# Gated attention and a three-layer sign network: layer three as seven products of half blocks, three of its weight sums on GpSimd

## The chip, the cores and the metric

The kernel runs on one core of one Trainium2 chip. The metric is device time in microseconds for the whole program, the median of several executions. Beside them one execution was profiled; every row below is from that one. The engines are TensorE (PE, its weight loads PEld), VectorE (DVE), ScalarE (ACT), GpSimd (POOL) and SyncE (SP), which issues nearly all DMAs here. Each takes its own instructions strictly in order and is tied to the others by semaphores.

## The reference

The input x is 4096 tokens of 512 features (2 x 2048), the context 256 keys (2 x 128). In short:

```python
x = x + tanh(g_xattn) * attention(layernorm(x), ctx, ctx)      # 16 heads of 32, 128 keys
h = concatenate([y, -y])                                       # y = layernorm(x)
h = 2 * relu(s0 * h @ sign(k0))                                # 1024 -> 2048
h = 2 * relu(s1 * h @ sign(k1))                                # 2048 -> 2048
out = x + tanh(g_ffn) * s2 * h @ sign(k2)                      # 2048 -> 512
```

The three weight matrices hold only +1 and -1 (from booleans), so they and small sums of them are exact in fp8. Activations are split into two fp16 parts, high and low, and each product is two matmuls into the same bank.

## The kernel before

Tokens go in 16 chunks of 256 (`CHUNKS`), of two tiles of 128 (`TT`). For a chunk f, layer one (L0) makes 2048 rows of H in 8 pairs (`PAIRS`), layer two ("L1", 2048 x 2048, weights W1) works in 4 groups (`GROUPS`) of 512 outputs, and layer three ("L2", 2048 x 512, weights W2) adds each group's share into two output banks. While chunk f goes through the network, the attention of chunk f+1 is woven in: `SLOTS` lists the steps of a chunk in order, and `WEAVE` and `QUERIES` say after which slot an attention item comes. Every engine walks through the same list and does its own part of each slot, first the slot's (`feed`), then the woven items (`attend`). So the list is the order of the work on all engines, written by hand.

From chunk 1 on, layer two is computed by a seven-product scheme (Strassen's, in Winograd's form): a group of 512 outputs times 256 tokens is split in 2 x 2 blocks; seven products P1, P2, P6, P5, P7, P4, P3 of half blocks (32 matmuls of 128 columns each, L1255 and L1256) replace eight. Its sums of weights (S1 to S4) are made once on VectorE in `weight_step` (L983 to L997); its sums of activations are made for each pair in layer one (L870 to L875, after which ScalarE makes the high part, `pair_hi`, L618, and VectorE the low one, `pair_lo`, L839). Its results are gathered in C11, C12 and C22: ScalarE copies a running bank (`take`, L622), VectorE adds another bank (`add`, L844), ScalarE rectifies into the high part of h1 (L667, L677, L680, L685) and VectorE makes the low part (`h1_rest`, L852). TensorE may only add on to a bank when the copy of it is done (`l1_copy`).

Layer three is plain before: for each group and half of the group's tiles (`second_feed`, L1272 and L1273), 8 matmuls of 512 columns, 64 a chunk; two banks (3 and 4) hold the output of the two token tiles over the whole chunk, and `finish` (L907) adds them to the kept x once a chunk. The share of the last group falls into the next chunk's slots (L2P).

An attention item S is the scores of 4 heads (L1167): VectorE takes the maximum (L804), ScalarE the exponents (4 instructions, L529), and in item PS its high part (L607), VectorE the low part (L808), SyncE sends both through a DMA transpose. PV is the product with the values (L1132, L1133), VectorE scales it (L815, L817) and GpSimd adds its two halves (L476). CT, WO, N2, T2 are the output projection and the second layernorm, LN, N1, T1 the first layernorm of the chunk after next, Q and QS the queries. Items use banks 5 to 7 in turn.

The order that ties an item to its neighbours on an engine:

```python
for f in range(CHUNKS):
    for s, slot in enumerate(SLOTS):
        feed(slot, f)
        ...
        if f < CHUNKS - 1:
            for ahead, item in woven(s, f):
                attend(item, f + ahead)
```

## Time and profile before

| | us |
|---|---|
| median of 3 runs | 1567.62 (1564.46 to 1568.11) |
| the profiled execution | 1564.91 |
| its span, first to last instruction | 1563.1 |
| TensorE busy | 1518.9 (97%), 19872 matmuls, granted clock 1.00 |
| VectorE busy | 940.2 (60%) |
| ScalarE busy | 673.7 (43%) |
| GpSimd busy | 168.7 (11%) |
| chunk 7, first layer-one matmul to that of chunk 8 | 92.66 |

A row such as `L839 DVE TENSOR_TENSOR H<-Fp,H 128x896 f16<-128x896 f32 x120 | 130.1, 1084 | 0.0` is a group of instructions: line, engine, operation, what it writes and reads, shapes, count, then busy us and mean ns of one, then the idle time before them and who ended it. In a timeline the first number is the start in us, the second the duration. Instructions of one engine overlap in their fill and drain, so the distance from start to start is shorter than the duration: for throughput one reads the starts. A matmul's duration is modelled and far longer than its distance to the next.

### The profile page before, as it was taken

How to read it: one execution, taken by the hardware profiler on the slowest of the kernel's cores; microseconds unless marked ns; L12 is line 12 of the kernel's file. 1: busy time of each engine (PE TensorE's matmuls, PEld its weight loads, DVE VectorE, ACT ScalarE, POOL GpSimd, SP SyncE). 2: the span in 40 equal slices, each digit the busy share in tenths (PEclk: the TensorE clock that was granted, in tenths of full speed). 3: DMA queues.
4: the chain of work that ended last, by engine and by line, in shares of the span. 5: the costliest groups of instructions: out<-in, count | busy, mean ns of one | idle time of the engine just before them, and what ended most of it. 6: DMA issues, size and time to landing. Idle time of an engine off the chain costs nothing.

```text
span 1563.1 us, 46137 instructions
## 1 busy us (share of the span) xinstructions
PE 1518.9 (97%) x19872; PEld 1297.3 (83%) x19872; DVE 940.2 (60%) x1938; ACT 673.7 (43%) x1568; POOL 168.7 (11%) x273
## 2 busy tenths in 40 slices
PE   6798999999999999999999999999999999999999
PEld 4586888888888888898988888888898888889887
DVE  5877766756556565655656566465655656565442
ACT  3452452635435253452535445263553525345231
POOL 2202001010100102011020200101010010201000
PEclk9999999999999999999999999999999999999999
DMA  9443232342424333252443524333242443424100
GB/s 256 127 104 58 46 95 62 89 70 62 90 52 101 65 85 78 50 100 55 96 69 71 93 44 103 62 89 69 62 90 52 101 67 83 78 50 100 29 29 15
DMA packets 278227, 120.96 MB, mean 77 GB/s; under 512 B 243464, under 2 KB 259848, under 8 KB 277896
## 3 DMA queue, kind: packets, MB, share of 16 engines
q1 hardware_dynamic: 275960, 117.48, 34.6%
q8 instruction: 157, 2.57, 0.7%
q10 hardware_dynamic: 2064, 0.53, 0.1%
q14 instruction: 46, 0.38, 0.1%
HBM read 37.76 MB, written 16.78 MB: 35 GB/s over the span
## 4 chain that ended last, share of the span: by engine, by line
PE 80%; DVE 8%; ACT 6%; issue 3%; DMA 2%; POOL 0%; SPq 0%; ACTq 0%; DVEq 0%; POOLq 0%
PE bank L1255 19%; PE bank L1256 19%; PE bank L1222 7%; PE bank L1223 7%; PE bank L1272 6%; PE bank L1273 6%; ACT Pf L529 3%; DVE nmax L804 2%; PE bank L1139 2%; PE bank L1141 2%; PE bank L1140 2%; PE bank L1123 2%; PE bank L1124 2%; PE bank L1125 2%; DMA PT<-Phl 1%
## 5 line engine op out<-in xcount | busy, mean ns | idle before, releaser
L1255 PE MATMUL bank<-H,W 128*128 128x128 f16 x6720 | 778.3, 219 | 5.7 <-ACT C L622 4.4
L1256 PE MATMUL bank<-H,W 128*128 128x128 f16 x6720 | 778.0, 219 | 0.0
L1255 PEld LDWEIGHTS bank<-H,W 128*128 128x128 fp8e5 x6720 | 655.3, 98 | 18.1 <-ACT C L622 10.2
L1256 PEld LDWEIGHTS bank<-H,W 128*128 128x128 fp8e5 x6720 | 657.4, 98 | 7.1
L1222 PE MATMUL bank<-hT,W 128*128 128x256 f16 x1024 | 226.8, 273 | 3.5 <-DVE hT L745 1.9
L1223 PE MATMUL bank<-hT,W 128*128 128x256 f16 x1024 | 226.8, 273 | 0.0
L529 ACT ACTIVATE Pf<-bank,nmax 128x128 f32<-128x128 f32 x512 | 146.4, 368 | 137.1 <-DVE nmax L804 135.4
L1273 PE MATMUL bank<-W,h 128*128 128x512 fp8e5 x504 | 191.0, 379 | 0.0
L1272 PE MATMUL bank<-W,h 128*128 128x512 fp8e5 x504 | 191.0, 379 | 0.0
L476 POOL TENSOR_TENSOR attn<-pvs 128x128 f32<-128x128 f32 x120 | 75.0, 625 | 1002.9 <-DVE pvs L817 1002.9
L844 DVE TENSOR_TENSOR C<-bank,C 128x256 f32<-128x256 f32 x180 | 76.3, 424 | 159.4 <-ACT C L622 87.8
L622 ACT ACTIVATE C<-bank 128x256 f32<-128x256 f32 x180 | 69.9, 388 | 211.3 <-PE bank L1256 211.3
L808 DVE SCALAR_TENSOR_TENSOR Phl<-Pf,Phl 128x512 f16<-128x512 f32 x120 | 82.6, 688 | 93.5 <-ACT Phl L607 93.5
L839 DVE TENSOR_TENSOR H<-Fp,H 128x896 f16<-128x896 f32 (+1 forms) x128 | 135.3, 1059 | 0.8 <-ACT H L613 0.8
L647 ACT ACTIVATE Fp<-bank 128x512 f32<-128x512 f32 x128 | 76.5, 597 | 90.0 <-PE bank L1223 88.7
L618 ACT ACTIVATE H<-Fp 128x896 f16<-128x896 f32 x120 | 113.4, 945 | 1.8 <-DVE Fp L875 1.7
L852 DVE SCALAR_TENSOR_TENSOR h<-C,h 128x256 f16<-128x256 f32 x180 | 77.3, 430 | 60.7 <-ACT h L685 29.0
L1222 PEld LDWEIGHTS bank<-hT,W 128*128 128x128 fp8e5 x1024 | 100.2, 98 | 15.4 <-issue 4.0
L1223 PEld LDWEIGHTS bank<-hT,W 128*128 128x128 fp8e5 x1024 | 100.2, 98 | 11.4
L804 DVE TENSOR_REDUCE nmax<-bank 128x4 f32<-128x512 f32 x128 | 87.6, 684 | 17.3 <-PE bank L1167 16.3
L1273 PEld LDWEIGHTS bank<-W,h 128*128 128x128 f16 x504 | 49.3, 98 | 50.4
L1272 PEld LDWEIGHTS bank<-W,h 128*128 128x128 f16 x504 | 49.3, 98 | 50.5
(133 smaller groups left out, 1910.3 us busy)
## 6 DMA issues: line engine op xcount, KB each, us to landing
Qst<-q_bounce SPq DMA_DIRECT2D x120, 128.0 KB, 2.8
Y<-in_x_dram SPq DMA_DIRECT2D x16, 512.0 KB, 3.9
R<-X SPq DMA_DIRECT2D x16, 512.0 KB, 3.5
q_bounce<-Qhl SPq DMA_DIRECT2D x120, 64.0 KB
out_dram<-R SPq DMA_DIRECT2D x15, 512.0 KB, 2.6
W<-in_L_ffn_k_dram SPq DMA_DIRECT2D x8, 512.0 KB, 8.1
W<-in_L_ffn_k_dram SPq DMA_DIRECT2D x2, 1024.0 KB, 19.3
PT<-Phl SPq DMA_TRANSPOSE x120, 3.1
```

What stands on the lines that cost most here:

```text
L529: last = nc.scalar.activation(Pf[:, n % 2, j * P:(j + 1) * P], bank[:, j * P:(j + 1) * P], ACT.Exp, bias=nmax[:, n % 2, j:j + 1], scale=1.0)
L618: nc.scalar.activation(H0[:, 0, i], Fp[:, i % 3, 1:8, :], ACT.Copy).then_inc(l0_hi, 1)
L804: V_.tensor_reduce(nmax[:, n % 2, :], bank[:, :].rearrange("p (j k) -> p j k", j=4), AX.X, ALU.max, negate=True).then_inc(s_max, 1)
L808: V_.scalar_tensor_tensor(out=Phl[:, n % 2, 1, :], in0=Pf[:, n % 2, :], scalar=PS, in1=Phl[:, n % 2, 0, :], op0=ALU.mult, op1=ALU.subtract)\
L839: V_.tensor_tensor(H0[:, 1, i, rows, :], Fp[:, i % 3, of, :], H0[:, 0, i, rows, :], ALU.subtract)\
L852: V_.scalar_tensor_tensor(out=h1_part(q, half, late, 1), in0=source, scalar=0.0, in1=h1_part(q, half, late, 0), op0=ALU.max, op1=ALU.subtr ...
L1222: mm(o, w, hT[:, k, :], start=k == 0, stop=False)
L1223: last = mm(o, w, hT[:, KT + k, :], start=False, stop=k == KT - 1)
L1255: mm(o, w, H0[:, 0, i, b_of, :], start=first, stop=False, skip_group_check=True)
L1256: last = mm(o, w, H0[:, 1, i, b_of, :], start=False, stop=i == PAIRS - 1, skip_group_check=True)
L1272: mm(banks[3 + t][:, :], hi, w2, start=q == 0 and h == 0 and jj == 0, stop=False)
L1273: last = mm(banks[3 + t][:, :], lo, w2, start=False, stop=q == GROUPS - 1 and h == 1 and jj == 1)
```

## The change

Layer three takes the seven-product form too. From chunk 1 on, the outputs of layer two are kept as seven blocks of sums (h1 becomes `[P, 2, 2, 2, 7, HALF]`), and a pass over two groups is seven steps (`PASS`) of 8 matmuls of 256 columns (`third_step`). Passes stand in the new list of slots: pass 1 of a chunk (groups 2 and 3) among the next chunk's layer-one slots 4 to 15, pass 0 (groups 0 and 1) in slots 31 to 42 between layer-two steps. After a step VectorE adds one or two halves of the bank to the kept x (`add_up`, 8 reads a pass), in place of `finish`. For each group VectorE makes three sums (`group_sums`) at the end of the group, ScalarE the high parts (`group_hi`, 1280 and 512 elements) and VectorE the low parts (`group_lo`) at the start of the next group, all in two of the three Fp buffers that layer one uses. Within a group the last two products change places (P3, P4), C12 gets a second add, and the three banks rotate from group to group (`ROLES`). W2 gets 7 blocks; of its four sums three are made by GpSimd (`third_sum`: S3, S2, S4, each 2048 elements a partition) at slots 12 to 14 of chunk 1 in GpSimd's own order, and S1 by VectorE at slot 17 (`third_first`). In chunk 0 layer three stays plain, and in the last chunk for its last two groups.

To make room, Kst holds the keys of one batch at a time (restacked at the start of chunk 7), Pf has one buffer instead of two, attn shares xn, Qf shares pvs, and ident shares C11. The woven items move to new slots.

```diff
     STEPS = [(A_L11, B_R11, A, True), (A_L12, B_R21, B, True), (A_S2, B_T2, A, False),
-             (A_S1, B_T1, C, True), (A_S3, B_T3, A, False), (A_L22, B_T4, A, False),
-             (A_S4, B_R22, C, False)]
-    P1, P2, P6, P5, P7, P4, P3 = range(7)
+             (A_S1, B_T1, C, True), (A_S3, B_T3, A, False), (A_S4, B_R22, B, True),
+             (A_L22, B_T4, A, False)]
+    P1, P2, P6, P5, P7, P3, P4 = range(7)
+    ROLES = [[(q + role) % 3 for role in range(3)] for q in range(GROUPS)]
+    H_R11, H_R22, H_T1, H_T3, H_T2, H_R21, H_T4 = range(7)
+    EARLY_ROWS, LATE_ROWS = slice(0, 5), slice(5, 7)
+    PASS = [(A_L11, H_R11), (A_L12, H_R21), (A_S2, H_T2), (A_S1, H_T1), (A_S3, H_T3), (A_S4, H_R22), (A_L22, H_T4)]
+    PASS_BANK = [3, 4, 3, 4, 3, 4, 3]
+    READS = [(P1, 0, 1), (P2, 0, 1), (P6, 0, 0), (P5, 1, 0), (P5, 0, 0), (P7, 1, 0), (P3, 0, 0), (P4, 1, 1)]
+    PASS_NEEDS = [0, 0, 1, 2, 3, 5, 6]
+    READ_NEEDS = [0, 1, 0, 0, 3, 4, 5, 0]
+    PLAIN_FEED = {0: {0: (0, 0), 1: (0, 1), 3: (1, 0), 4: (1, 1)}, 1: {0: (2, 0), 1: (2, 1), 2: (3, 0), 3: (3, 1)}}
...
+    LAST_FEED = [(0, 1, 0), (1, 0, 1), (0, 0, 2), (1, 1, 3)]
+    SLOTS = [("L0", i, 0) for i in range(4)]
+    for n in range(4):
+        SLOTS += [("L2", 1, n), ("L0", 4 + n, 0)]
+    SLOTS += [("L2", 1, P7), ("L2", 1, P3), ("L1", 0, P1), ("L2", 1, P4)] + [("L1", 0, s) for s in range(P2, 7)]
+    SLOTS += [("L1", 1, s) for s in range(7)] + [("L1", 2, P1), ("L1", 2, P2)]
+    for n, s in enumerate((P6, P5, P7, P3)):
+        SLOTS += [("L2", 0, n), ("L1", 2, s)]
+    SLOTS += [("L2", 0, P7), ("L2", 0, P3), ("L1", 2, P4), ("L2", 0, P4)] + [("L1", 3, s) for s in range(7)]
...
+    for u, (scores, values) in enumerate(((14, 20), (17, 22), (19, 24), (21, 26), (23, 28), (25, 31), (27, 33),
+                                          (29, 36))):
+        weave(scores, "S", u)
+        weave(scores + 1, "PS", u)
+        weave(values, "PV", u)
     for t in range(TT):
-        weave(28 + 2 * t, "CT", t)
-        weave(31 + 2 * t, "WO", t)
-        weave(32 + 2 * t, "N2", t)
-        weave(33 + 2 * t, "T2", t)
-    weave(31, "LOAD", 0)
+        weave(34 + 3 * t, "CT", t)
+        weave(40 + 2 * t, "WO", t)
+        weave(41 + 2 * t, "N2", t)
+        weave(42 + 2 * t, "T2", t)
...
+    THIRD_SUMS = {12: 1, 13: 2, 14: 3}
...
-        W2 = sb("W2", [P, FT, D], f8)
+        W2 = sb("W2", [P, 7, PAIRS, D // 2], f8)
...
+            def third_sum(step):
+                L11, L12, L21, L22 = (W2[:, b] for b in range(4))
+                if step == 1:
+                    pool.wait_ge(w2_made, 1)
+                    pool.tensor_tensor(W2[:, A_S3], L11, L21, ALU.subtract, saturate=False).then_inc(w2_sums, 1)
+                if step == 2:
+                    pool.wait_ge(w2_sums, 1)
+                    pool.tensor_tensor(W2[:, A_S2], L22, W2[:, A_S3], ALU.subtract, saturate=False)\
+                        .then_inc(w2_sums, 1)
+                if step == 3:
+                    pool.wait_ge(w2_sums, 2)
+                    pool.wait_ge(l2_done, 2 * GROUPS)
+                    pool.wait_ge(w2_first, 1)
+                    pool.tensor_tensor(W2[:, A_S4], L12, W2[:, A_S2], ALU.subtract, saturate=False)\
+                        .then_inc(w2_sums, 1)
...
+            def group_hi(q, f):
+                for n, rows in enumerate((EARLY_ROWS, LATE_ROWS)):
+                    act.wait_ge(h2_step, 3 * group(f, q) + 2 + n)
+                    if n == 0:
+                        act.wait_ge(*pass_free(f, q))
+                    nc.scalar.activation(h1[:, q % 2, 0, :, rows, :], Fp[:, 1:3, rows.start + 1:rows.stop + 1, :],
+                                         ACT.Copy).then_inc(h2_hi, 1)
...
-                        take(n, s, f, C11, A)
+                        if n > 0 and not late(f, n - 1):
+                            group_hi(n - 1, f)
+                        if late(f, n - 1):
+                            act.wait_ge(h1_lo, NH + 1)
+                        take(n, s, f, C11)
...
+            def group_sums(q, f):
+                done = 3 * group(f, q)
+                Fg = Fp[:, 1:3]
+                dve.wait_ge(h2_relu, 3 * group(f, q) + 3)
+                V_.tensor_tensor(Fg[:, :, 3:5, :], Fg[:, :, 1:3, :], Fg[:, :, 0:1, :].to_broadcast([P, 2, 2, HALF]),
+                                 ALU.subtract).then_inc(h2_step, 1)
+                dve.wait_ge(h2_step, done + 1)
+                V_.tensor_tensor(Fg[:, :, 5, :], Fg[:, :, 4, :], Fg[:, :, 1, :], ALU.add).then_inc(h2_step, 1)
+                dve.wait_ge(h2_step, done + 2)
+                dve.wait_ge(l1_copy, copied(f, q, 3))
+                V_.tensor_tensor(Fg[:, :, 7, :], Fg[:, :, 6, :], Fg[:, :, 5, :], ALU.subtract).then_inc(h2_step, 1)
+            def group_lo(q, f):
+                for n, rows in enumerate((EARLY_ROWS, LATE_ROWS)):
+                    dve.wait_ge(h2_hi, 2 * group(f, q) + n + 1)
+                    V_.tensor_tensor(h1[:, q % 2, 1, :, rows, :], Fp[:, 1:3, rows.start + 1:rows.stop + 1, :],
+                                     h1[:, q % 2, 0, :, rows, :], ALU.subtract).then_inc(h2_lo, 1)
+            def add_up(f, p, s):
+                base = NR * passes(f, p)
+                for n, (step, half, tile) in enumerate(READS):
+                    if step != s:
+                        continue
+                    if n == 0 and p == 0:
+                        dve.wait_ge(r_copied, nth(f, 16, 15))
+                    if READ_NEEDS[n]:
+                        dve.wait_ge(l2_sum, base + READ_NEEDS[n])
+                    dve.wait_ge(l2_step, 7 * passes(f, p) + s + 1)
+                    rest = R[:, tile, half * CHUNK:(half + 1) * CHUNK]
+                    V_.scalar_tensor_tensor(out=rest, in0=banks[PASS_BANK[s]][:, 0:CHUNK], scalar=fin, in1=rest,
+                                            op0=ALU.mult, op1=ALU.add).then_inc(l2_sum, 1)
...
+                    if s == P4 and not late(f, n):
+                        group_sums(n, f)
...
+            def third_first():
+                V_.scalar_tensor_tensor(out=W2[:, A_S1], in0=W2[:, 2], scalar=-1.0, in1=W2[:, 3], op0=ALU.mult,
+                                        op1=ALU.subtract, saturate=False).then_inc(w2_first, 1)
...
-                        pe.wait_ge(l1_sum, nth(f - 1, NC, 3 * (n - 1) + 2))
+                        pe.wait_ge(l1_copy, copied(f, n, 0))
...
                     if s == P7:
-                        pe.wait_ge(l1_copy, nth(f - 1, NC, 3 * n + 1))
+                        pe.wait_ge(l1_copy, copied(f, n, 1))
...
+            def third_step(f, p, s):
+                base = NR * passes(f, p)
+                block, row = PASS[s]
+                if s == P1 and base == 0:
+                    pe.wait_ge(out_ready, NT)
+                elif s == P1:
+                    pe.wait_ge(l2_sum, base)
+                if PASS_NEEDS[s]:
+                    pe.wait_ge(l2_sum, base + PASS_NEEDS[s])
+                if f == 1 and p == 0 and s == P6:
+                    pe.wait_ge(w2_sums, 2)
+                if f == 1 and p == 0 and s == P5:
+                    pe.wait_ge(w2_first, 1)
+                if f == 1 and p == 0 and s == P3:
+                    pe.wait_ge(w2_sums, 3)
+                if s in (P1, P2):
+                    pe.wait_ge(h2_lo, 2 * group(f, 2 * p + 1) + 1 + s)
+                for q in (2 * p, 2 * p + 1):
+                    for i in range(2):
+                        for hl in range(2):
+                            last = mm(banks[PASS_BANK[s]][:, 0:CHUNK], h1[:, q % 2, hl, i, row, :],
+                                      W2[:, block, 2 * q + i, :],
+                                      start=s in (P1, P2, P5, P3) and q == 2 * p and i == hl == 0,
+                                      stop=q == 2 * p + 1 and i == hl == 1, skip_group_check=True)
+                last.then_inc(l2_step, 1)
...
+                    if kind == "L2" and f - q >= 1:
+                        third_step(f - q, q, h)
+                    if kind == "L2" and f - q == 0 and h in PLAIN_FEED[q]:
+                        second_feed(*PLAIN_FEED[q][h], 0)
```

## Rows read from the trace of the kernel before

**Rows 1.** The page, busy time: us (share of the span) x instructions.

```profile
PE 1518.9 (97%) x19872; PEld 1297.3 (83%) x19872; DVE 940.2 (60%) x1938; ACT 673.7 (43%) x1568; POOL 168.7 (11%) x273
```

**Rows 2.** Busy time by stretch: us, then each engine; chunk 7 and chunk 1.

```profile
734.57:753.79 19.22, 19.22 (x180) 17.22 (x178) 14.91 (x33) 12.95 (x22) 0.00 (x0) 1.00 0.15 42
757.23:785.59 28.36, 28.05 (x469) 25.80 (x468) 15.73 (x34) 14.42 (x42) 2.57 (x4) 1.00 0.57 109
734.57:827.23 92.66, 92.35 (x1259) 79.62 (x1257) 55.37 (x118) 41.94 (x98) 9.79 (x16) 1.00 0.41 77
175.37:269.39 94.02, 92.67 (x1256) 79.65 (x1257) 63.61 (x120) 41.67 (x97) 9.81 (x16) 1.00 0.33 77
```

**Rows 3.** The waits of TensorE: waited for, us in total, times, longest.

```profile
PE bank L1255 <- ACT C L622: 4.4, 15, 0.6
```

**Rows 4.** Groups by line and form, whole run: busy, mean ns, idle before.

```profile
L1273 PE MATMUL bank<-W,h 128*128 128x512 fp8e5 x504 | 191.0, 379 | 0.0
...
L839 DVE TENSOR_TENSOR H<-Fp,H 128x896 f16<-128x896 f32 x120 | 130.1, 1084 | 0.0
...
L618 ACT ACTIVATE H<-Fp 128x896 f16<-128x896 f32 x120 | 113.4, 945 | 1.8 <-DVE Fp L875 1.7
...
L446 POOL TENSOR_TENSOR X<-Y,bo_b 128x512 f32<-128x512 f32 x32 | 40.5, 1267 | 0.4 <-DVE bo_b L950 0.4
...
L987 DVE TENSOR_TENSOR W<-W 128x2048 fp8e5<-128x2048 fp8e5 x4 | 9.1, 2284 | 0.0
```

**Rows 5.** Timeline of TensorE, four places: start us, us, instruction.

```profile
72.10 0.27 PE L1223 MATMUL bank<-hT,W 128*128 128x256 f16 x1
72.20 0.27 PE L1222 MATMUL bank<-hT,W 128*128 128x256 f16 x1
...
706.40 0.38 PE L1272 MATMUL bank<-W,h 128*128 128x512 fp8e5 x1
706.62 0.38 PE L1273 MATMUL bank<-W,h 128*128 128x512 fp8e5 x1
...
762.82 0.39 PE L1167 MATMUL bank<-Kst,Qst 128*128 128x128 f16 x4
763.04 0.22 PE L1255 MATMUL bank<-H,W 128*128 128x128 f16 x1
...
766.61 0.39 PE L1167 MATMUL bank<-Kst,Qst 128*128 128x128 f16 x4
```

**Rows 6.** Timeline with GpSimd; then line 792 by tile (ns min/median/max).

```profile
783.94 0.42 DVE L817 TENSOR_TENSOR pvs<-bank,rden 128x256 f32<-128x256 f32 x1
784.28 0.68 DVE L808 SCALAR_TENSOR_TENSOR Phl<-Pf,Phl 128x512 f16<-128x512 f32 x1
784.44 0.83 POOL L476 TENSOR_TENSOR attn<-pvs 128x128 f32<-128x128 f32 x1 [5.29 <-DVE pvs L817]
784.88 0.69 DVE L804 TENSOR_REDUCE nmax<-bank 128x4 f32<-128x512 f32 x1
...
L792 DVE TENSOR_TENSOR xs<-attn,xs x30: 679/693/1083, 140.4 to 1451.1; 128x512 f16<-128x512 f32 x30
```

**Rows 7.** Timeline of VectorE and ScalarE around two score blocks.

```profile
763.73 0.68 DVE L804 TENSOR_REDUCE nmax<-bank 128x4 f32<-128x512 f32 x1
764.45 1.14 ACT L529 ACTIVATE Pf<-bank,nmax 128x128 f32<-128x128 f32 x4 [0.99 <-DVE nmax L804]
765.63 0.63 ACT L607 ACTIVATE Phl<-Pf 128x512 f16<-128x512 f32 x1
766.29 0.69 DVE L808 SCALAR_TENSOR_TENSOR Phl<-Pf,Phl 128x512 f16<-128x512 f32 x1 [1.87 <-ACT Phl L607]
...
774.10 1.14 ACT L529 ACTIVATE Pf<-bank,nmax 128x128 f32<-128x128 f32 x4 [1.09 <-DVE nmax L804]
775.12 0.40 ACT L622 ACTIVATE C<-bank 128x256 f32<-128x256 f32 x1
775.38 0.66 ACT L607 ACTIVATE Phl<-Pf 128x512 f16<-128x512 f32 x1
```

374 lines of the change are left out of this document (219 added, 155 removed).

## Prediction

> **What bounds the kernel now.** I read the busy table first [rows 1], then busy time by stage [rows 2], then who made TensorE wait [rows 3]. One steady chunk (chunk 7) takes 92.66 us and TensorE is busy for 92.35 of them; the 13 chunks from 2 to 14 are alike. TensorE is the bound. In the whole run its waits on ScalarE for a layer-two copy come to 4.4 us; I count 0.25 a chunk. So every matmul column that goes is worth its time, as long as VectorE and ScalarE still keep up. They look idle over a chunk (55 and 42 us of 92.66), but the stages differ: in the layer-one stretch VectorE is busy 14.91 of 19.22 us, and in the stretch with the scores it and ScalarE do 15.73 and 14.42 of 28.36 us, largely one after the other [rows 2].
>
> **What the change removes from TensorE.** Layer three is 64 matmuls of 512 columns a chunk (1024 in all, half of them in the row of L1273 and the rest in its twin and the tail) [rows 4]. One follows the other after 0.22 us (0.2156 over a long stretch) [rows 5]. A seven-product pass over two groups is 7 steps of 8 matmuls of 256 columns; such matmuls follow each other after 0.11 us (0.1091) [rows 5]. That they move fp8 weights changes nothing that the 512-column rows show. So 64 x 0.2156 = 13.80 us becomes 112 x 0.1091 = 12.22: 1.58 us less in each of chunks 1 to 14, and half of that in chunk 15; chunk 0 stays plain. 14 x 1.58 + 0.8 = **22.9 us less**.
>
> **What it adds, and by what price.** Start to start, without a wait: VectorE 0.34 us for 256 elements and 0.60 for 512 [rows 6], for 896 it lasts 1.08 [rows 4], start to start some 0.08 less as in the others, 1.00; so I estimate 1.40 for 1280. ScalarE: 0.26 to 0.3 for 256 [rows 7], and from 0.94 us for 896 [rows 4] about 1.16 for 1280 and 0.53 for 512. For each group VectorE loses four rests of 0.34 and gains one add (0.34), three group sums (0.73, 0.46, 0.36 with their hand-overs: 1.55), group_lo (1.40 + 0.60 = 2.0) and four reads of a product out of PSUM (4 x 0.36); finish goes (1.2 a chunk). That is 14 us more per chunk: 55 becomes about 69 of 91, still under TensorE. ScalarE gains group_hi, 1.16 + 0.53 = 1.69 a group, 7 us a chunk. By totals alone both would hide. Where they stand in the order decides.
>
> **The layer-one stretch** (slots 0 to 13). TensorE now needs 8 x 16 matmuls (1.745 us each time) for layer one, 4 x 12 (1.31) for the queries and 7 x 8 (0.87) for layer three, all of 256 columns: 25.3 us up to the end of the third step there. VectorE needs group_lo 2.0, eight pairs at 2.0, four query rests at 0.36, seven reads at 0.36: 22 us, but starts only when ScalarE has done group_hi, about 2 us in. Followed in order, the last low half of H is there 0.15 us before TensorE asks for it. I put it at nothing, with up to 1 us a chunk as upper bound; nothing to be gained. The cover is gone in chunk 15, where the queries (5.2 us) aren't there: 1 us net.
>
> **The score stretch** (slots 14 to 31), the heart of the forecast. A score block is a chain over both engines, read in [rows 7]: maximum to exponents 0.72 (763.73 to 764.45), exponents to their copy 1.18, copy to the low half 0.66, and 0.60 for that [rows 6]. If other work of ScalarE stands behind the exponents, it starts 1.02 after them (774.10 to 775.12). A step of layer two is 1.785 us, a score 0.22 (762.82 to 763.04; 762.82 to 766.61 is one score and two steps) [rows 5], a value product about 0.25 (8 matmuls of 65 columns, 0.03 each by the same pace).
> First wait: after score 3 (slot 21) VectorE does the group sums (1.55), then the maximum (0.73), ScalarE the exponents (1.02), and only then, since group_hi stands ahead of the copy of C11 in slot 22, group_hi (1.69) and the copy with its signal (0.38): 5.4 us. The product P6 in slot 24 adds to the bank that is copied and waits for it. TensorE has 2 steps, a score and a value product until there, 4.04 us. **1.35 us of waiting.**
> Second: from the start of group_hi, its first half (1.3), group_lo (2.0), the value scaling (0.55), the low half of score 3 (0.60), the add of C11 (0.34), the maximum of score 4 (0.73), exponents (1.02) and the copy of C12 (0.4) are 6.95 us; TensorE is through P6 and P5 6.15 us after that same start. P7 waits **0.8 us**.
> Third: two more score blocks take 3.65 and 4.0 us, about TensorE's own pace (4.04 for two slots), so nothing is caught up. After score 6 come its exponents (1.75), the rectified copy (0.45), the group sums (1.55), a value scaling (0.55), the low half (0.60) and the first part of group_lo (1.5): 6.4 us. The first step of layer three for groups 0 and 1 (slot 31) reads that part. TensorE gets there first by **2.05 us**.
> After slot 31 the layer-three steps and the output projection stretch TensorE's side, and I find no further wait above 0.1 us. Sum: 4.2 us a chunk, against 0.25 before [rows 3]. Bounds: 2.5 if each new long operation is a fifth cheaper than I took it, 5.0 if dearer. 13 x (4.2 - 0.25) = **51.4 us more**. The new waits of TensorE hold back the whole queue behind them, scores included, and VectorE, which depends on that queue, gains nothing by them.
>
> **Chunk 1 and the weight sums.** It now takes 94.02 us, 1.6 of that waits [rows 2]. VectorE's own sum for layer three (slot 17) and the layer-two weight sums in slots 13 and 25 stand in the same chain, each 2.3 us by the 2048-element row [rows 4]; by the same walk some 5.5 us of them come out on top of 4.2. 9.7 - 1.65 = **8 us more**. The three sums on GpSimd: its 512-element sum takes 1.27 us [rows 4], so 2048 elements are at most 5.1 us, 15 us in all. Two can start in chunk 0, right behind the last layernorm (GpSimd waits for no slot); the third waits for slot 17 of chunk 1 and is wanted in slot 40, over 30 us later. TensorE never waits for them. What is queued behind the third is the first value sum, wanted by VectorE four slots on; covered. But the two engines stop each other: a GpSimd sum beside VectorE's low half took 0.83 us [rows 6] and ended 0.39 after that one had drained, and a VectorE subtraction that takes 0.69 took up to 1.08 [rows 6]. If every GpSimd sum held VectorE for its whole length it would be 15 us, if it waited for gaps 0; I take **2 us**, nearest to the 0.4 of these rows, a few times. The Trainium skill ("GPSIMD Engine Reference", section Specifications) says that GpSimd's SBUF interface is shared with VectorE and contended when VectorE has two SBUF inputs; the rows agree. Its section "Performance versus the Vector engine" gives 4.5 us for a two-input addition over 2048 elements, twice VectorE's time, and advises against moving such work there; by its figure the three would be 13.5 us of GpSimd, once, and the forecast would stay.
>
> The rest is at nothing: the keys stacked for one batch at a time (the second batch goes out at the start of chunk 7, 14 slots ahead of its first score), W2 in two loads of the size of the layer-two loads, the shared buffers (Pf alone, since the low half of one score precedes the next maximum on VectorE anyway). Chunk 0's order changes with stalls of about 8 us in it; 3 either way.
>
> **Sum.** The profiled execution is 1564.9 us with its span of 1563.1; the median of the runs is 2.7 above, 0.2%. 1564.9 - 22.9 + 51.4 + 8 + 2 + 1 = 1604.4; I say 1605.
>
> **Rivals.** (a) All is covered: the hand-overs are shorter than the chain I built from single rows, and TensorE goes through. 1564.9 - 22.9 = 1542, with a few us of chunk 1 about 1545. For it: both engines have over 20% of idle time, and in the kernel before the same chain leaves TensorE 0.25 us of waiting a chunk. Against it: it does so with no sums and no group_hi or group_lo between the scores. (b) Half of it: only about half of the 4.2 us is seen, the waits being one slack spent once: some 1573. The break-even is at 1.8 us of waiting a chunk, and below it the sign turns. (c) More: VectorE also binds in the layer-one stretch by 1 us a chunk, or GpSimd holds it: 1620 to 1635. (d) The columns don't come back (256-column steps with overhead of their own, each step closed by a signal): at most 0.05 us a step, 10 us; within (b) or (c).
>
> **Chances.** My case 0.60 (1590 to 1618), (a) 0.20, (b) 0.10, (c) 0.10. Below 1546 I leave about 0.1, above 1622 about 0.08. About 0.3% (5 us) is what a measurement of this kernel can tell from no change. Faster 0.20 is (a); same 0.05 and slower 0.05 share (b); with my case and (c), slower is 0.75.
>
> **What would show it.** In the profile after, TensorE's matmul count and busy time in a chunk fall by the layer-three share while its chunk is 94 to 96 us long; its waits name ScalarE's copy of C (before P6 and P7 of the second group) and VectorE's group_lo (before the first step of layer three), each once a chunk, of 1.3, 0.8 and 2 us. Wrong if the steady chunk is near 91 us, if those waits are absent, or if the longest wait names W2.

## The result and the profile after

The kernel after takes **1647.2 us** (median of 4 runs, 1646.8 to 1648.4), the kernel before beside it 1567.3 us. The ratio is **1.0514** (interval 1.0496 to 1.0533), 80 us more. The forecast was 1605. The profiled execution of after has a span of 1645.5 us, 82.4 more than that of before.

First the page's busy times, then groups of the view by line and form: those of the layer-three products, of the reads out of PSUM (L1004), of group_lo (L989) and of group_hi (L736).

```profile
PE 1518.5 (92%) x20568; PEld 1374.8 (84%) x20568; DVE 1162.9 (71%) x2262; ACT 762.9 (46%) x1684; POOL 201.7 (12%) x276
...
L1458 PE MATMUL bank<-W,h 128*128 128x256 fp8e5 x1624 | 207.5, 274 | 28.7 <-DVE h L989 28.2 <-DVE R L1004 0.5
L1004 DVE SCALAR_TENSOR_TENSOR R<-bank,c,R 128x256 f32<-128x256 f32 x232 | 107.0, 477 | 15.9 <-PE bank L1458 15.6
L989 DVE TENSOR_TENSOR h<-Fp,h 128x1280 f16<-128x1280 f32 x58 | 89.6, 1545 | 46.9 <-ACT h L736 46.9
L736 ACT ACTIVATE h<-Fp 128x1280 f16<-128x1280 f32 x58 | 73.7, 1270 | 18.3 <-DVE Fp L981 18.3
L989 DVE TENSOR_TENSOR h<-Fp,h 128x512 f16<-128x512 f32 x58 | 39.6, 682 | 0.0
L736 ACT ACTIVATE h<-Fp 128x512 f16<-128x512 f32 x58 | 36.0, 620 | 0.0
```

TensorE's share fell from 97% [rows 1] to 92%: it is no longer the bound throughout. VectorE has 223 us more. Next, busy time by stretch, cut where layer one of each chunk begins: of after the prologue, chunks 0, 1, 7, 8 and 15.

```profile
0.00:74.75 74.75, 49.45 (x329) 35.69 (x330) 48.60 (x114) 28.14 (x73) 18.21 (x35) 0.95 0.69 190
74.75:184.35 109.60, 91.92 (x841) 76.01 (x841) 86.98 (x113) 36.05 (x81) 17.85 (x18) 0.96 0.33 68
184.35:293.52 109.17, 95.56 (x1280) 82.99 (x1281) 76.72 (x134) 45.57 (x103) 15.45 (x17) 0.98 0.26 61
780.44:877.30 96.86, 91.68 (x1304) 84.28 (x1305) 69.89 (x140) 48.16 (x107) 11.61 (x16) 1.00 0.38 78
877.30:975.32 98.02, 92.98 (x1304) 85.93 (x1305) 69.80 (x140) 48.11 (x107) 11.64 (x16) 0.98 0.35 72
1556.99:1645.50 88.51, 84.16 (x1171) 76.30 (x1168) 45.12 (x90) 28.16 (x51) 0.00 (x0) 1.00 0.05 20
```

And of before the three of these stretches that [rows 2] doesn't have: prologue, chunk 0, chunk 15.

```profile
0.00:71.77 71.77, 46.54 (x328) 34.57 (x329) 48.47 (x114) 28.15 (x73) 18.25 (x35) 1.00 0.72 197
71.77:175.37 103.60, 95.72 (x856) 77.52 (x857) 80.62 (x113) 36.10 (x81) 14.13 (x16) 1.00 0.36 76
1477.23:1563.10 85.87, 81.78 (x1107) 70.30 (x1104) 31.22 (x66) 23.49 (x45) 0.00 (x0) 1.00 0.05 20
```

So the 82.4 us lie here: prologue +3.0, chunk 0 +6.0, chunk 1 +15.2, chunks 2 to 14 +55.6 (4.3 each), chunk 15 +2.6. The last number but two of a row is the granted clock. It was 1.00 in every stretch of the profiled execution of before (all but one of the other runs of before whose clock was noted have a mean of 0.996 to 0.998); in after it is 0.95 to 0.98 in the first three rows and in chunks 2, 4, 8, 10 and 12, which last 98.0 us (chunk 10 98.7). Below, an undisturbed chunk is one at clock 1.00 without the odd longer wait for a transfer; several of each kernel agree within 0.05 us, in after at 96.4.

TensorE's waits, in the columns of [rows 3]:

```profile
PE bank L1430 <- ACT C L719: 35.4, 44, 3.2
PE bank L1458 <- DVE h L989: 28.2, 14, 2.6
PE bank L1396 <- DVE h L1010: 13.0, 1, 13.0
PE bank L1396 <- DVE C L962: 9.9, 13, 0.8
```

The first two are the forecast ones: copies of C by ScalarE, and group_lo by VectorE before layer three. The third is a single wait, ahead of chunk 1. The fourth, of each chunk's first step on the last add of C, was not forecast. In the timeline of TensorE in chunk 7 a wait is seen so; the number in brackets is the idle time:

```profile
823.69 0.39 PE L1341 MATMUL bank<-Kst,Qst 128*128 128x128 f16 x4
825.27 0.23 PE L1430 MATMUL bank<-H,W 128*128 128x128 f16 x1 [1.20 <-ACT C L719]
...
842.33 0.38 PE L1458 MATMUL bank<-W,h 128*128 128x256 fp8e5 x2 [1.86 <-DVE h L989]
...
876.32 0.22 PE L1431 MATMUL bank<-H,W 128*128 128x128 f16 x1
877.30 0.27 PE L1396 MATMUL bank<-hT,W 128*128 128x256 f16 x1 [0.76 <-DVE C L962]
```

Without a wait the step after a score starts 0.22 us after it [rows 5]; here it is 1.58, so 1.36 us are lost and not the 1.20 in the brackets. The idle time is counted from the modelled end of the last matmul, so each wait costs some 0.16 us more than it (0.25 idle in before's chunk 7 is 0.42 start to start). Below, "lost" is start to start, less the usual distance.

### The profile page after: what moved, and what is told of

Its sections match the earlier page's. It is cut to its first block, busy times and chain, and to the rows that moved or that the text cites. A ratio compares the mean times of both kernels' runs of the same rounds, so it can differ in the third digit from the quotient of the medians.

```text
span 1645.5 us, 48159 instructions
## 1 busy us (share of the span) xinstructions
PE 1518.5 (92%) x20568; PEld 1374.8 (84%) x20568; DVE 1162.9 (71%) x2262; ACT 762.9 (46%) x1684; POOL 201.7 (12%) x276
## 3 DMA queue, kind: packets, MB, share of 16 engines
q8 instruction: 162, 2.65, 0.7%
## 4 chain that ended last, share of the span: by engine, by line
PE 55%; DVE 22%; ACT 10%; issue 7%; POOL 3%; DMA 2%; SPq 0%; DVEq 0%; ACTq 0%; POOLq 0%
PE bank L1458 10%; PE bank L1430 10%; PE bank L1431 10%; PE bank L1396 6%; PE bank L1397 6%; ACT Pf L623 4%; DVE nmax L922 3%; DVE h L989 3%; DVE Phl L926 2%; DVE C L962 2%; PE bank L1313 2%; PE bank L1315 2%; PE bank L1314 2%; PE bank L1297 2%; ACT xs L688 2%
## 5 line engine op out<-in xcount | busy, mean ns | idle before, releaser
L1430 PE MATMUL bank<-H,W 128*128 128x128 f16 x6720 | 790.9, 220 | 38.1 <-ACT C L719 35.4
L1431 PE MATMUL bank<-H,W 128*128 128x128 f16 x6720 | 790.2, 220 | 0.0
L1396 PE MATMUL bank<-hT,W 128*128 128x256 f16 x1024 | 230.5, 274 | 24.8 <-DVE h L1010 13.0
L1458 PE MATMUL bank<-W,h 128*128 128x256 fp8e5 x1624 | 207.5, 274 | 28.7 <-DVE h L989 28.2
L1397 PE MATMUL bank<-hT,W 128*128 128x256 f16 x1024 | 230.5, 274 | 0.0
L551 POOL TENSOR_TENSOR xn<-pvs 128x128 f32<-128x128 f32 x120 | 72.1, 601 | 1031.0 <-DVE pvs L935 1031.0
L1458 PEld LDWEIGHTS bank<-W,h 128*128 128x128 f16 x1624 | 154.0, 98 | 47.7 <-issue 30.2
L962 DVE TENSOR_TENSOR C<-bank,C 128x256 f32<-128x256 f32 x240 | 100.4, 418 | 106.2 <-ACT C L719 53.2
L989 DVE TENSOR_TENSOR h<-Fp,h 128x1280 f16<-128x1280 f32 x116 | 124.5, 1114 | 46.9 <-ACT h L736 46.9
L728 ACT ACTIVATE Fp<-C 128x256 f32<-128x256 f32 x174 | 72.8, 418 | 133.3 <-DVE C L962 133.3
L1004 DVE SCALAR_TENSOR_TENSOR R<-bank,c,R 128x256 f32<-128x256 f32 x232 | 107.0, 477 | 15.9 <-PE bank L1458 15.6
L736 ACT ACTIVATE h<-Fp 128x1280 f16<-128x1280 f32 x116 | 103.8, 945 | 18.3 <-DVE Fp L981 18.3
```

Source lines behind the costliest of these rows:

```text
L962: V_.tensor_tensor(to[:, :, :], banks[bank][:, 0:CHUNK].rearrange("p (j n) -> p j n", j=2), to[:, :, :], ALU.add).then_inc(l1_sum, 1)
L989: V_.tensor_tensor(h1[:, q % 2, 1, :, rows, :], Fp[:, 1:3, rows.start + 1:rows.stop + 1, :], h1[:, q % 2, 0, :, rows, :], ALU.subtract).th ...
L1004: V_.scalar_tensor_tensor(out=rest, in0=banks[PASS_BANK[s]][:, 0:CHUNK], scalar=fin, in1=rest, op0=ALU.mult, op1=ALU.add).then_inc(l2_sum, 1)
L1396: mm(o, w, hT[:, k, :], start=k == 0, stop=False)
L1397: last = mm(o, w, hT[:, KT + k, :], start=False, stop=k == KT - 1)
L1430: mm(o, w, H0[:, 0, i, b_of, :], start=first, stop=False, skip_group_check=True)
```

## The waits of a steady chunk

Lost in chunk 7: 1.36 us before P6 of group 1, 0.81 before its P7, 2.02 before the first layer-three step; then 0.45 before P4 of group 3, 0.92 before the next chunk's first step, 0.46 for the queries' transposed input and 0.28 for that of a value product. The chain behind the first two, ScalarE and VectorE in the timeline of chunk 7:

```profile
822.12 1.14 ACT L623 ACTIVATE Pf<-bank,nmax 128x128 f32<-128x128 f32 x4 [1.89 <-DVE nmax L922]
823.14 1.80 ACT L736 ACTIVATE h<-Fp 128x1280 f16<-128x1280 f32 x2
824.82 0.40 ACT L719 ACTIVATE C<-bank 128x256 f32<-128x256 f32 x1
...
829.68 0.40 ACT L719 ACTIVATE C<-bank 128x256 f32<-128x256 f32 x1
...
824.46 2.09 DVE L989 TENSOR_TENSOR h<-Fp,h 128x1280 f16<-128x1280 f32 x2 [2.37 <-ACT h L736]
...
827.02 0.68 DVE L926 SCALAR_TENSOR_TENSOR Phl<-Pf,Phl 128x512 f16<-128x512 f32 x1
827.62 0.42 DVE L962 TENSOR_TENSOR C<-bank,C 128x256 f32<-128x256 f32 x1
```

Exponents at 822.12, group_hi at 823.14, and only at 824.82 the copy for which TensorE waits; group_lo from 824.46 to 826.47 ahead of the low half and the add of C11 (827.62), which stand ahead of the next maximum and the next copy (829.68). Link by link it is the forecast's chain.

Four experiments try it. **a4** takes the first link out of TensorE's way:

```diff
-                        if n > 0 and not late(f, n - 1):
-                            group_hi(n - 1, f)
...
                         take(n, s, f, C11)
+                        if n > 0 and not late(f, n - 1):
+                            group_hi(n - 1, f)
```

> The kernel after, with ScalarE's group_hi behind the copy of C11 instead of ahead of it. Theory A, one chain over ScalarE and VectorE sets the pace of the score stretch: the wait before P6 of group 1 (1.2 us idle) goes, the one before P7 grows from 0.65 to about 2.0, and the total stays at 1647 within 5 us. Theory B, each wait is a local collision: the 1.2 us wait goes in 13 chunks and nothing grows, 1647 - 18 = 1629 us (1625 to 1634).

Measured: 1669.1 us, ratio 1.0653 (1.0636 to 1.0670): 22 us **more** than after. In chunk 8 the wait before P6 is gone, and the next one is

```profile
935.44 0.23 PE L1430 MATMUL bank<-H,W 128*128 128x128 f16 x1 [2.29 <-ACT C L719]
...
977.03 0.23 PE L1430 MATMUL bank<-H,W 128*128 128x128 f16 x1 [1.12 <-ACT C L719]
```

2.29 us idle where there were 1.20 and 0.65: the whole of the first wait went into the second, as theory A has it, and a little more. The second row, in group 3, is new, and neither theory had it. ScalarE shows why:

```profile
970.59 0.38 ACT L719 ACTIVATE C<-bank 128x256 f32<-128x256 f32 x1 [2.49 <-PE bank L1431]
970.87 1.78 ACT L736 ACTIVATE h<-Fp 128x1280 f16<-128x1280 f32 x2
```

It stands idle for 2.49 us until TensorE has done P1, and group_hi, ready long before, starts only behind the copy. The waits are parts of one chain; taking the first link out of it by this edit moves the waiting and adds to it.

**b1** moves the other end, the reader of group_lo, by one layer-two step:

```diff
-    SLOTS += [("L1", 1, s) for s in range(7)] + [("L1", 2, P1), ("L1", 2, P2)]
-    for n, s in enumerate((P6, P5, P7, P3)):
+    SLOTS += [("L1", 1, s) for s in range(7)] + [("L1", 2, s) for s in (P1, P2, P6)]
+    for n, s in enumerate((P5, P7, P3, P4)):
         SLOTS += [("L2", 0, n), ("L1", 2, s)]
-    SLOTS += [("L2", 0, P7), ("L2", 0, P3), ("L1", 2, P4), ("L2", 0, P4)] + [("L1", 3, s) for s in range(7)]
+    SLOTS += [("L2", 0, s) for s in (P7, P3, P4)] + [("L1", 3, s) for s in range(7)]
```

> The kernel after, with the layer-three pass over groups 0 and 1 begun one layer-two step later (behind P6 of group 2; at its end three of its steps follow each other). The first step then finds group_lo 1.8 us further on. Theory A, that wait stands alone (nothing behind it is late): 13 x 1.8 = 23 us less, and if the half-clock stretches that follow it in about half of the chunks go with it, 10 us more: 1614 us (1608 to 1625). Theory B, the chain over ScalarE and VectorE carries on and the same time is waited at another step: 1642 or more. The runs of after vary by some us with the number of half-clock stretches.

Measured: 1633.2 us, 1.0419 (1.0403 to 1.0434), 14 us less than after: between the two theories. Chunk 8 by stretch, then its one new wait:

```profile
871.05:966.57 95.52, 91.44 (x1304) 84.35 (x1305) 69.78 (x140) 47.88 (x107) 11.09 (x16) 1.00 0.35 73
```

```profile
931.23 0.23 PE L1430 MATMUL bank<-H,W 128*128 128x128 f16 x1 [0.88 <-ACT C L719]
```

The 2 us wait is gone, and 0.88 us idle comes in its place before P6 of group 2, the same collision as in group 1, which had been hidden by the longer wait. Undisturbed chunks last 95.5 instead of 96.4, and none of chunks 2 to 14 has a clock below 1.00 any more: the second half of theory A.

**b2** and **c3** measure the price of the splits by leaving most of them out, from chunk 2 on:

```diff
                 for n, rows in enumerate((EARLY_ROWS, LATE_ROWS)):
+                    if f > 1:
+                        rows = slice(rows.start, rows.start + 1)
```

in group_hi and group_lo (b2), in group_lo alone (c3).

> The kernel after, with group_hi and group_lo cut to one row each instead of five and two, from chunk 2 on (the rest of the fp16 pairs of layer three is left out, so the output isn't the reference's). Theory A, the length of these four operations a group makes the three waits of the score stretch: they shrink to about 0.5 a chunk together, 13 x 3.6 = 47 us less and 10 of clock: 1590 us (1580 to 1602). Left are the two waits at the chunk's end and the matmul columns. Rival, the group sums and hand-overs alone keep the waits: 1620 or more.

> The kernel after with only VectorE's group_lo cut to one row each from chunk 2 on (the low parts of the other rows are left out, so the output isn't the reference's), ScalarE's group_hi whole. Cutting both gave 1581.5, 65 less than after. Theory A, one chain in which the two follow each other: each counts by its length (1.4 us of VectorE, 1.0 of ScalarE in a group), so 35 to 40 us go: 1610 us (1600 to 1622). Theory B, VectorE alone is what is short: 1590 or less. Theory C, ScalarE's group_hi, which stands ahead of the copies, makes the waits: 1630 or more.

Measured: b2 1581.5 us, 1.0090 (1.0075 to 1.0106); c3 1595.2 us, 1.0170 (1.0155 to 1.0185). A steady chunk of b2, then one of c3:

```profile
846.13:938.40 92.27, 90.92 (x1304) 84.36 (x1305) 64.96 (x140) 44.21 (x107) 10.30 (x16) 1.00 0.38 77
```

```profile
854.07:947.37 93.30, 90.91 (x1305) 84.35 (x1306) 65.05 (x140) 48.37 (x107) 10.30 (x16) 1.00 0.37 76
```

b2 came out as its theory A said, c3 between its theories A and B. 66 us of the 80 hang on these operations: 52 on VectorE's group_lo, of which some 4.8 us a chunk were cut (69.8 to 65.1 busy), and 14 more on group_hi with 4.2 us cut (48.4 to 44.2). My theory A gave group_lo 35 to 40. About 8 of the 52 are clock: the five slow chunks are gone in both runs. Even without them a us of VectorE weighed about three times a us of ScalarE, in this order of cutting; group_hi cut alone was not tried. The waits at the chunk's end, which I hadn't laid to the splits at all, nearly went with them: of the 13 waits of a chunk's first step, 9.9 us idle in after, b2 has 3 with 1.5 us, and the one before P4 of group 3 is gone. b2's chunk 8 has two waits left, 0.79 us idle before layer three and 0.13 for a copy. b2's fastest chunks last 91.83 us, 0.8 less than before's: the columns do come back.

Two attempts at a better order, on top of b1. **c1** puts the second, two-row part of group_hi behind the copy of C11 and that of group_lo behind the add; **c2** also sets the scores apart from the group sums of slot 21:

```diff
-    for u, (scores, values) in enumerate(((14, 20), (17, 22), (19, 24), (21, 26), (23, 28), (25, 31), (27, 33),
-                                          (29, 36))):
+    for u, (scores, values) in enumerate(((14, 20), (16, 22), (18, 24), (20, 26), (23, 28), (25, 31), (27, 33),
+                                          (30, 36))):
```

> The kernel with the layer-three pass begun one step later, and in it the second, two-row part of group_hi behind the copy of C11 and that of group_lo behind the add of C11 (0.53 and 0.60 us that stood ahead of them). Theory A, the chain over ScalarE and VectorE is waited for link by link, so what leaves its front comes off the waits before P6 and P7: 0.5 to 1 us a chunk, 7 to 12 us below the run with the later pass (1633): 1623 us (1617 to 1628). Theory B, the chain is as long as before, only in another order: 1631 to 1635.

> The same as the run with the late part, and scores 1 to 3 one slot earlier, the last one slot later, so that no score is made in the slot of a group's sums (21). Theory A: the score blocks and the splits collide by their place; apart, another 1 to 2 us a chunk goes: 1608 us (1597 to 1618). Theory B: VectorE is late out of the layer-one stretch already, and earlier scores only wait there: 1620 or more.

Measured: c1 1621.4 us, 1.0341 (1.0324 to 1.0358); c2 1610.5 us, 1.0269 (1.0251 to 1.0286). Both fall where theory A put them; undisturbed chunks last 94.7 and 94.0 us. So part of the loss was order: 2.4 of the 3.75 us by which an undisturbed chunk of after exceeds before's 92.66.

## The end of the chunk

Chunk 7's tail, in the timeline of VectorE, shows the layernorm of a later chunk (L904, L913) ahead of the last add of C (L962), for which the next chunk's first step at 877.30 waits:

```profile
874.89 0.54 DVE L904 TENSOR_SCALAR xn<-Y,mv,rstd 128x512 f32<-128x512 f32 x1
...
876.13 0.69 DVE L913 SCALAR_TENSOR_TENSOR xs<-xn,xs 128x512 f16<-128x512 f32 x1 [0.36 <-ACT xs L688]
876.74 0.41 DVE L962 TENSOR_TENSOR C<-bank,C 128x256 f32<-128x256 f32 x1
```

**b3** takes it two slots forward (and orders two buffers by waits for what is long done):

```diff
-    weave(39, "LOAD", 0)
+    weave(37, "LOAD", 0)
     for t in range(TT):
-        weave(43 + t, "LN", t, 2)
-        weave(45 + t, "N1", t, 2)
-        weave(46 + t, "T1", t, 2)
+        weave(41 + t, "LN", t, 2)
+        weave(43 + t, "N1", t, 2)
+        weave(44 + t, "T1", t, 2)
```

> The kernel after, with the next chunk's layernorm, its splitting and its load two slots earlier (slots 41 to 45 instead of 43 to 47). In chunk 7 of after these stand ahead of the copy of C22 on ScalarE and of the last adds on VectorE, where TensorE waits 0.46 before P4 and 0.92 before layer one (start to start). Theory A: both waits go and the wait for the queries' transpose at the chunk's start too: 13 x (1.4 to 1.8) = 18 to 24 us less, 1625 us (1620 to 1631). Rival, the last adds are late by their own chain, or the work moved only makes layer-two steps of group 3 wait: 1643 or more.

Measured: 1663.2 us, 1.0610 (1.0585 to 1.0634), 16 us more. The wait at the chunk's start is gone; instead two steps of group 3 wait 1.29 and 0.69 us idle in chunk 7 where one waited 0.29. The rival was right. **d1** leaves the work where it is and changes which bank is wanted first:

```diff
-                                         banks[(n + 1) % 3][:, :].rearrange("p (b n) -> p b n", b=4), ACT.Relu)\
+                                         banks[(2 - n) % 3][:, :].rearrange("p (b n) -> p b n", b=4), ACT.Relu)\
...
-                    if n == 0 and f >= 2:
-                        pe.wait_ge(l1_sum, nth(f - 2, NC, NC - 1))
+                    if n < 2 and f >= 2:
+                        pe.wait_ge(l1_sum, nth(f - 2, NC, NC - 2 + n))
```

> The kernel after, with the banks of layer one taken in the order 2, 1, 0 instead of 1, 2, 0, so that a chunk's first step needs the add of C22 (after P7 of group 3) and not the last add of C12. Theory A, the wait of 0.92 us (start to start) at each chunk's start is the hand-over of that one bank, freed 1.4 us too late because the next chunk's layernorm stands ahead of the last adds: it goes, 13 x 0.92 = 12 us less, 1635 us (1630 to 1640). Theory B, VectorE is simply behind at the chunk's end, and the time is waited a step later: 1644 or more.

Measured: 1637.6 us, 1.0444 (1.0422 to 1.0465), 10 to 11 us less than after, undisturbed chunks 95.7: theory A, with 0.7 instead of 0.92 a chunk. That wait was one bank freed late.

## GpSimd's sums

The end of chunk 0 in the timeline of after, VectorE, then GpSimd:

```profile
169.09 4.03 DVE L904 TENSOR_SCALAR xn<-Y,mv,rstd 128x512 f32<-128x512 f32 x1 [1.08 <-POOL rstd L529]
173.05 5.91 DVE L1163 TENSOR_TENSOR W<-W 128x2048 fp8e5<-128x2048 fp8e5 x1
...
169.02 3.82 POOL L559 TENSOR_TENSOR W<-W 128x2048 fp8e5<-128x2048 fp8e5 x1
172.92 3.88 POOL L562 TENSOR_TENSOR W<-W 128x2048 fp8e5<-128x2048 fp8e5 x1
```

The first sum starts 0.07 us ahead of VectorE's layernorm step and the second 0.13 ahead of its weight sum. **a1** leaves the three sums out (loaded bytes stand in their place):

```diff
-                    if f == 1 and s in THIRD_SUMS:
-                        third_sum(THIRD_SUMS[s])
```

> The kernel after, with the three layer-three weight sums of GpSimd left out (the blocks they would write hold loaded bytes, so the output isn't the reference's; one more load of 0.5 MB in the prologue fills them). Theory 1: while a GpSimd sum of 2048 elements runs (3.8 us), VectorE stands still, so the two sums at the end of chunk 0 make most of TensorE's 13.0 us wait before chunk 1. Then the wait falls to 2 to 5 us, chunk 1 gives back 2 to 5 more, and the total is some 13 us below the kernel after: 1634 us (1630 to 1638). Rival: the wait comes from VectorE's own layer-two weight sums there, and the GpSimd sums cost next to nothing: 1643 or more.

and the same two instructions of VectorE are

```profile
168.00 0.55 DVE L904 TENSOR_SCALAR xn<-Y,mv,rstd 128x512 f32<-128x512 f32 x1 [1.09 <-POOL rstd L531]
168.46 2.28 DVE L1163 TENSOR_TENSOR W<-W 128x2048 fp8e5<-128x2048 fp8e5 x1
```

3.5 and 3.6 us shorter, each by nearly a whole sum: VectorE stood still while GpSimd worked. TensorE's idle time before chunk 1 falls from 13.0 to 5.9 us, chunk 0 from 109.6 to 102.0, chunk 1 from 109.2 to 108.6. Total 1641.5 us, 1.0464 (1.0445 to 1.0482). That is 6 to 8 us less and not 13: by the two chunks the sums cost 8.2 us, of which 3 more disturbed chunks than in after (eight of chunks 2 to 14 instead of five) took some back. The mechanism of theory 1 stands, its size for chunk 1 doesn't.

**a3** makes the second sum twice, one instruction more behind it:

```diff
+                    pool.wait_ge(w2_sums, 2)
+                    pool.tensor_tensor(W2[:, A_S2], L22, W2[:, A_S3], ALU.subtract, saturate=False)\
+                        .then_inc(w2_sums, 1)
```

> The kernel after, with the second GpSimd sum made twice (the same result). Theory 1: one more sum of 3.9 us at the same place adds its whole length to the wait before chunk 1 (13.0 becomes 17): 1651 us (1650 to 1653). Rival, GpSimd's sums are hidden beside VectorE and only the first overlap hurts: 1647 to 1648.

Measured: 1653.3 us, 1.0548 (1.0529 to 1.0567), 6 us more than after. The idle time before chunk 1 is 16.7 us, 3.6 more, and chunk 0 lasts 113.4: theory 1. Here it is GpSimd that gives way in its turn:

```profile
176.29 5.75 POOL L565 TENSOR_TENSOR W<-W 128x2048 fp8e5<-128x2048 fp8e5 x1
```

5.75 us for a sum that takes 3.9 alone. **c4** cuts each sum into four instructions:

```diff
+                for i in range(0, PAIRS, 2):
+                    last = pool.tensor_tensor(to[:, i:i + 2], a[:, i:i + 2], b[:, i:i + 2], ALU.subtract,
+                                              saturate=False)
```

> The kernel after with each GpSimd sum in four instructions of 512 elements. Theory A, the two engines exclude each other for whole instructions, and either gets in between the other's: VectorE waits at most 1 us at a time, but as often, and the same 7 to 8 us are lost at the end of chunk 0: 1647 us (1643 to 1652), the idle time before chunk 1 11 to 15 us. Theory B, a short GpSimd instruction runs beside VectorE nearly unhindered, as the 512-element ones of the kernel before seemed to: the idle time before chunk 1 falls to about 6 us and the total to 1640.

```profile
169.09 13.82 POOL L556 TENSOR_TENSOR W<-W 128x512 fp8e5<-128x512 fp8e5 x8
...
169.17 1.30 DVE L908 TENSOR_SCALAR xn<-Y,mv,rstd 128x512 f32<-128x512 f32 x1 [1.09 <-POOL rstd L529]
170.39 3.18 DVE L1167 TENSOR_TENSOR W<-W 128x2048 fp8e5<-128x2048 fp8e5 x1
```

Now the engines take turns: each VectorE instruction shown is 0.75 to 0.9 us longer than alone, about one piece, and the eight pieces last 13.8 us instead of 7.7. The idle time before chunk 1 is 10.3 us, chunk 0 2.7 us shorter; the total, 1646.6 us (1.0499, 1.0476 to 1.0523), can't be told from after's. Theory A, for whole instructions, with a little less lost.

**a2** undoes the GpSimd part of the change alone, the same sums on VectorE:

```diff
-    THIRD_SUMS = {12: 1, 13: 2, 14: 3}
+    THIRD_SUMS = {12: 1, 14: 2, 18: 3}
...
+                    V_.tensor_tensor(W2[:, A_S3], L11, L21, ALU.subtract, saturate=False).then_inc(w2_sums, 1)
```

> The kernel after, with the same three sums on VectorE (slots 12, 14 and 18 of chunk 1), the GpSimd part of the change undone alone. Theory 1: three sums of 3.8 us in which VectorE stands still are replaced by three of 2.3 us of VectorE's own, and they leave the end of chunk 0: the 13.0 us wait falls to 2 to 5 us, chunk 1 becomes up to 6 us longer. Total 1638 us (1632 to 1643). Rival: GpSimd takes work off VectorE, as one would hope: 1650 to 1655.

Measured: 1644.7 us, 1.0490 (1.0474 to 1.0505). Chunks 0 and 1 together are 218.8 us in after, 210.6 without the sums, 214.7 here: GpSimd's cost 8.2, VectorE's 4.1. In total 2.5 to 4 us are gained, not the 9 that I expected, and the total lies outside both ranges: in chunk 1 TensorE now waits 5.9 us at once for a copy of C, where after has 1.5. **b4** instead makes two sums in slots 24 and 31 of chunk 0 and takes the last layer-two weight sums of chunk 0 3 to 6 slots forward, with the edits of b1 and b3:

```diff
-    THIRD_SUMS = {12: 1, 13: 2, 14: 3}
+    THIRD_SUMS = {(0, 24): 1, (0, 31): 2, (1, 14): 3}
```

> The kernel after with three edits: the layer-three pass begun one step later, the next chunk's layernorm two slots earlier, and in chunk 0 GpSimd's first two sums made in slots 24 and 31 and VectorE's last layer-two weight sums 4 to 5 slots earlier, so that neither stands at its end. If the three are independent, the gains add: 33 + 22 + 12 = 67 us less than after, 1580 us (1570 to 1595). If the waits are parts of one chain, the first two give less than their sum: 1600 to 1620.

Measured: 1638.6 us, 1.0457 (1.0440 to 1.0475). The idle time before chunk 1 is 1.63 us, as in before, but chunk 0 is only 2 us shorter: its value products and projections wait 2.2, 2.4 and 2.9 us idle now. VectorE probably has too much to do in chunk 0, so that moving it moves the wait. Neither theory: the gains don't add, and b3's part is a loss.

## The granted clock

Chunk 8 of after, three stretches around its third wait:

```profile
936.00:938.80 2.80, 0.67 (x12) 0.52 (x10) 2.80 (x4) 1.41 (x3) 0.83 (x1) 1.00 0.21 41
938.80:943.00 4.20, 4.20 (x44) 4.05 (x44) 2.49 (x6) 1.97 (x6) 0.00 (x0) 0.59 0.21 39
943.00:975.32 32.32, 31.26 (x448) 27.45 (x446) 21.86 (x44) 9.18 (x19) 8.23 (x11) 1.00 0.36 65
```

After 2.13 us of idle time the mean clock of the next 4.2 us is 0.59: TensorE works through most of them at 1.2 GHz instead of 2.4 and loses 1.6 us (98.02 against 96.41 for the chunk). To see whether the wait does it or something else in after, **d3** makes one in the kernel before, and **d4** a shorter one:

```diff
+                    if s == P4 and n == 1 and 2 <= f < CHUNKS - 1:
+                        pe.wait_ge(p_lo, nth(f + 1, NU, 6))
```

(p_ready in place of p_lo in d4).

> The kernel BEFORE with one wait more in chunks 2 to 14: P4 of group 1 also waits for the low half of score 6, which by its trace is some 2.3 us later. Nothing else is changed. Theory A, a wait of TensorE of 2 us brings a half-clock stretch of itself in about half of the chunks, as in after: 13 x 2.4 + 6 x 1.6 = 41 us more, 1608 us (1602 to 1616), clock 0.98 in some chunks. Theory B, the stretches of after come from something else in it (its denser small matmuls or its VectorE load): clock 1.00 throughout and 13 x 2.4 = 31 us more, 1598 us.

> The same with the wait for the exponents of score 6 instead, some 1.1 us. Both theories: clock 1.00 in chunks 2 to 14, as in the runs whose longest wait there was 1.2 us; 13 x 1.2 = 16 us more, 1583 us (1578 to 1588). With half-clock stretches here too, 1590 or more, and the length of the wait would not be what decides.

Measured: d3 1604.4 us, 1.0239 (1.0224 to 1.0254), d4 1582.3 us, 1.0097 (1.0080 to 1.0114). The waits of d3, and its chunks 4 and 5:

```profile
PE bank L1257 <- DVE Phl L808: 31.7, 13, 2.5
```

```profile
463.11:558.42 95.31, 92.75 (x1259) 79.79 (x1257) 55.42 (x118) 41.91 (x98) 9.78 (x16) 1.00 0.33 74
558.42:655.28 96.86, 94.06 (x1261) 81.26 (x1258) 55.43 (x118) 41.91 (x98) 9.78 (x16) 0.98 0.34 71
```

and of d4:

```profile
PE bank L1257 <- ACT Pf L529: 14.3, 13, 1.1
```

A wait of 2.2 to 2.5 us brought the slow stretch to steady chunks of the kernel before, which had none: theory A. In the profiled run it did so in 2 of 13 chunks, not in half (the total is near the expected one because each wait lost 2.65 us, not 2.4); the other three runs of d3 have mean clocks of 0.994, 0.993 and 0.989 against its 0.996, so probably more such stretches. With 1.1 us, none. The other kernels fit, by their profiled executions. Where a wait of 2 us stood in each of the chunks from 2 to 14 or nearly (after, a1 to a4, b3, c4, d1), 4 to 9 of them were slow; in b1, b2, c1, c3 and d4, whose longest wait there was 1.45 us, none. c2 has one slow chunk, and in it its longest wait, 1.98 us of a value product for its transpose; b4 has a wait of 1.99 us for a copy of C and d2 one of 1.96 for a transpose, and neither has a slow chunk. Longer waits don't always bring it either: in chunk 1 of after one of 3.24 us had clock 1.00 behind it, where b2, b3, b4 and d1 have a slow stretch behind theirs of 3.2. What decides was not found. The prologue's slow stretch (clock 0.95, 3 us) also came in d3 and d4, whose prologue is that of before, and not in b1: it isn't the change's.

## All that helped, in one kernel

**d2** joins b1, c1, c2, d1 and the sums on VectorE.

> All that helped in one kernel: the pass one step later, the late part of the splits behind the copy and add, the scores moved (1610), the three sums on VectorE (some 4 less) and the new bank order (some 12 less). If VectorE's and ScalarE's chain isn't what binds at these places: 1594 us (1588 to 1602). If the chain binds anyway: 1600 to 1610. Either way slower than the kernel before.

Measured: 1598.8 us, 1.0199 (1.0184 to 1.0214), undisturbed chunks 93.3 us. It came out within the range of the first case. 48 of the 80 us were order and place, with the clock that went with them. What is left, 32 us by the medians and 34 by the profiled executions, is 18.6 in chunk 1 (112.7 us, with one wait of 7.0), 8.6 in chunks 2 to 14, and the rest mostly in the prologue and the last chunk. No version tried comes down to the kernel before.

## Why the forecast was right on the waits that it walked, and short by half

The forecast was 39.5 us more, the profiled executions differ by 82.4: 43 us are missing. By stretch, forecast against the span of after: prologue 0 and +3.0; chunk 0 +2 and +6.0; chunk 1 +6.4 and +15.2; chunks 2 to 14 +30.9 and +55.6; chunk 15 +0.2 and +2.6.

**Layer-three columns, -22.9: right.** In each chunk 112 matmuls of 256 columns replace 64 of 512 and follow each other after 0.110 us in after (0.109 forecast); rival (d) falls. b2's fastest chunk is 0.83 us below before's and loses 1.24 us in its two waits, where before's loses 0.42: 1.65 us by that count, with 1.58 forecast. So nothing is left in a steady chunk for the shared buffers or the second add of C12. The sign "TensorE's matmul count falls" was wrong in itself: a chunk has 48 more matmuls, smaller ones (the rows of chunk 7 show 1259 and 1304). I overlooked only where they lie: after does half of a chunk's layer three in the next chunk and before a quarter, so chunk 0 loses 16 of its 512-column matmuls (3.5 us), and chunks 1 and 15 get 0.8 and 2.7 us more than I had given them. That is the +2.6 of the last one.

**The prices of the operations: right.** group_lo 2.0 forecast and 2.01 start to start, group_hi 1.69 and 1.68, group sums 1.55 and 1.52, a read of a product 0.36 and 0.39 at most.

**The three waits, 4.2 us: right, each by itself.** 1.35, 0.8 and 2.05 forecast, 1.36, 0.81 and 2.02 measured in chunk 7 (the third is 1.7 to 2.3 by chunk, 2.1 in the mean). Rivals (a) and (b), which let the idle time of both engines cover them, fall. I had set against them before's idle time of 0.25 [rows 3], though start to start that wait costs 0.42, a small slip in the other direction. The break-even of 1.8 us is 22.9 over 13 chunks and leaves out that 0.25 and the other terms of the sum; with them it is 1.2.

**"After slot 31 I find no further wait above 0.1": wrong.** This is the step that failed in the steady chunk, and the largest part of what is missing. I didn't walk the last slots, where the next chunk's layernorm and its splits stand ahead of the copy of C22 and of the last adds: 0.45 and 0.92 us a chunk, 18 us in 13 chunks. b2 shows that they come with the splits, though the splits' own place is elsewhere; d1 shows that the larger is one bank's order.

**The clock: left out.** Five slow chunks at 1.6 us, 8 us, and more in chunks 0 and 1. The forecast had a 2 us wait in every chunk, and that wait is what the slow stretches follow; all rows of before had 1.00, and I took no price for its loss. The Trainium skill ("TensorE: Matmul & The Clock Gate", section HAM oscillation) says that TensorE comes out of a long idle gap at the low clock, and means gaps longer than the 2.1 us here. By it these waits would have cost no clock; the runs show 1.6 us each, and only some of the time.

**GpSimd's sums, 2 us: wrong by a factor of four, within the bounds of 0 to 15.** The working chose the end of its range by the 0.4 us of [rows 6] (0.31 by the end of the low half; 0.39 is counted from the start of the next instruction). These are short instructions, and half of them met gaps: of the eight of L476 in chunk 7 of before, four took 0.45 us and four 0.65 to 0.83. That value was for a partial overlap; an instruction of VectorE that meets a 3.8 us sum waits for all of it. The length was right (at most 5.1, measured 3.82). The place was wrong: "right behind the last layernorm" is where VectorE has its last weight sums and the chunk's end hangs on it. The Trainium skill has the rule in a page that I didn't weigh ("SBUF — State Buffer", section Who interferes with whom): the pair of ports that the two engines share is held for the whole instruction, and the other blocks fully. The trace agrees, 4.03 and 5.91 us for 0.55 and 2.28. By it, an estimate, the first two sums would have cost their own 7.7 us; a1 gives 7.6 for chunk 0. The Trainium skill's "GPSIMD Engine Reference" (section Specifications), which I did weigh, names two conditions, two SBUF inputs or a two-port mode of VectorE; I used the first alone, and the layernorm step, with one tensor as input, was held as well.

**Chunk 0, otherwise: within its 3 us.** Without the sums it is 102.0 us (a1), 1.6 less than before, of which the moved columns are 3.5.

**Chunk 1, +6.4: wrong by 8.8.** Some 2 us are clock after the 13 us wait, 0.8 the columns. The rest is waits: 15.6 us lost, with the one that ends the chunk, where I had walked 9.7; 0.6 of the difference is GpSimd's third sum (a1). The longest are 3.2 us idle for a copy of C and 2.6 before layer three. Which of VectorE's weight sums makes which was not taken apart.

Rival (c), VectorE more of a bound than I had it, or GpSimd holding it, was right in kind; it lies at the chunk's end and in chunks 0 and 1, not in the layer-one stretch, where TensorE waits for nothing of VectorE in chunk 7, and at 1620 to 1635 it was priced too low as well.

## What to carry to other kernels

When a bound engine's waits are forecast by walking a chain, walk it once round the whole loop, past its end into the next turn: the three waits that were walked came out within 0.05 us in chunk 7, and the largest part of the error, 18 of 43 us, was in slots that weren't. An engine at 60% of the span has no 40% to give where its work is serial with another's; ask what a microsecond of it costs by cutting one, as c3 did, before moving work to it. And a wait removed alone at the front of a chain only moves down it (a4), while its reader moved back (b1) or the order changed (c1, c2, d1) gives time back.

## What the hardware showed that was not expected

GpSimd and VectorE excluded each other for whole instructions where both worked on SBUF tensors: a 0.55 us VectorE step took 4.03 us beside a GpSimd sum of 2048 fp8 elements (3.82 us), and a GpSimd sum took 5.75 us, 1.9 longer than alone, when a VectorE sum was under way. So GpSimd's three sums cost 8.2 us where VectorE's own cost 4.1. And a wait of TensorE of some 2 us now and then cost 1.6 us more after it had ended, at half clock (2 to 9 of 13 chunks in the profiled executions); one of 1.45 us or less never did in chunks 2 to 14.
